# Graph attention layer on one core: ScalarE's queue asks for the right halves of x after GpSimd's first constant, and the first weight slab is asked for after the second left half

## The chip, the cores and the metric

The program runs on one core of a Trainium2 chip. Its engines are TensorE (PE), VectorE (DVE), ScalarE (ACT), GpSimd (POOL) and SyncE (SP); transfers are asked for on the queues of SP, ACT and POOL and are all carried by the core's 16 DMA engines. The metric is device time in microseconds of one execution, as the median of several runs.

## What is computed

x has 384 rows (nodes) of 1024 features. The kernel normalises each row, applies relu, runs a graph attention layer with 16 heads on it and adds the result to x:

```
h = relu(layernorm(x))                                 # 384 x 1024
q, k, v = h @ wq.T + bq, h @ wk.T + bk, h @ wv.T + bv
q2, k2, v2 = q @ wiq.T + biq, k @ wik.T + bik, v @ wiv.T + biv     # split into 16 heads of 64
mask[src, dst] = softplus(edge_type_weights)[type - 1]  # -inf elsewhere, 6528 edges
attn = softmax(q2 @ k2.T / 8 + mask)
out = x + (attn @ v2) @ wo.T + bo
```

## The kernel before

The seven weight matrices come as 56 slabs of 128 x 1024 float32 (512 KB each), in the order in which TensorE uses them. Every slab and every activation is split into a high and a low part (w_hi, w_lo; a_hi, a_lo), and each product is three matmuls: high by high, low by high, high by low. ScalarE makes the high parts, VectorE or GpSimd the low ones. Each engine has its own program, written out by hand in order; semaphores tie them together, and nothing is scheduled by a planner.

The change touches the start alone, which runs so:

- SyncE (L286 on) asks for the left halves of x's three tiles, `x_sb[:, t, 0:512]`, 256 KB each (L289). Then follow the slabs (L305): slab 0 once the first left half has landed (L304); slab 1; then the weights of the edge types, the biases, the rows and columns of the edges (L307 to L312); slab 2; two fills of the table in memory that the mask is scattered into (`cells<-prob`, L316); slab 3 once slab 0 has been split; and so on, three raw slabs at a time.
- ScalarE (L450 on) asks for the three right halves of x (L470) as its first work. Then it loads a table, turns tiles 0 and 1 of x into h (relu with scale and bias, L476), makes the high part of the left half of slab 0 (L467), scales tile 2 in two quarter pieces (L482), and takes the eight turned blocks of h from PSUM as a_hi (L486), with slab 1's high part between (L456).
- GpSimd (L342 on) writes its constants: `iota` first (L345), which raises the semaphore iota_ok, then `above`, `ident` and others, and fills two blocks (L363). Then it raises each tile's variance to the power -1/2 (rstd, L367), and makes the low parts of slab 0 (L384) and slab 1 (L374).
- VectorE (L598 on) makes the statistics of each half of each tile as it lands (L679), left half first; the aggregate (L683) and the variance plus epsilon (L685) after both; and the shift of the tile before (L626) after the left half of the next. Of tile 2 it does the subtraction itself (L689, L693), converts the right half of slab 0 (L695), and makes a_lo (L725).
- TensorE (L845 on) waits for iota and above and runs 18 warming matmuls (L890), turns seven of the eight blocks of tile 0 (L894), runs 4 warming ones, turns tile 1, runs 3, turns tile 2, and starts the first tile of v (L922, L923, L929). After it come all other tiles and slabs (L849 to L851) and the heads.

Of the kernel before, what the change touches and what calls it, by code (L numbers as in the profile page):

```python
# [66 lines left out]
def tiles_of(group):  # L67
    return range(group * EG, min((group + 1) * EG, ET))


def gat_kernel(nc, slabs, x, edge_cols, edge_rows, edge_weights, biases, bo, out):
    with ExitStack() as ctx:
# [3 lines left out]
        def sem(name):  # L76
            return ctx.enter_context(nc.semaphore(name))
# [71 lines left out]
        def key_copy(pos):  # L149

            first, n = [(work2, 0), (work2, 4), (work2, 8), (work, 0), (work, 4), (work, 8), (prob, 19), (prob, 23),
                        (prob, 3), (prob, 7), (prob, 11), (prob, 15), (prob, 0)][pos], len(tiles_of(UNIT_ORDER[pos])) * P
            flat = prob[:, :, :, :].rearrange("p a t n -> p (a t n)") if first[0] is prob else first[0]
            return flat[:, first[1] * P:first[1] * P + n]

        def cell_rows(c):

            return cells[c][0:N * N, :].rearrange("(t p n) a -> p t (n a)", p=P, n=N)
# [18 lines left out]
        x_in = [[sem(f"x_in{t}_{b}") for b in range(2)] for t in range(NT)]  # L177
        slab_in = [sem(f"slab_in{r}") for r in range(RAW)]
        const_step, iota_ok, above_ok = sem("const_step"), sem("iota_ok"), sem("above_ok")
# [81 lines left out]
        def wait_lo(eng, s):  # L261

            eng.wait_ge(slab_lo_dve if lo_by_vector(s) else slab_lo, lo_count(s))
# [22 lines left out]
        @block.sync  # L286
        def _(sp_eng):
            for t in range(NT):
                sp_eng.dma_start(x_sb[:, t, 0:HALF], x[t * P:(t + 1) * P, 0:HALF]).then_inc(x_in[t][0], 16)  # L289
            def load_keys(pos):  # L290

                unit = UNIT_ORDER[pos]
                part = key_rows[0:1, unit * EG * P:(unit * EG + len(tiles_of(unit))) * P]
                sp_eng.dma_start(key_copy(pos), part.to_broadcast([P, len(tiles_of(unit)) * P])).then_inc(
                    keys_in[pos], 16)

            for s in range(SLABS):
                if s >= RAW:

                    wait_lo(sp_eng, s - RAW)  # L300
                    if s == RAW:
                        sp_eng.wait_ge(half_lo, 1)
                if s == 0:
                    sp_eng.wait_ge(x_in[0][0], 16)  # L304
                sp_eng.dma_start(raw[:, s % RAW, :], slabs[s]).then_inc(slab_in[s % RAW], 16)  # L305
                if s == 1:
                    sp_eng.dma_start(ew[:], edge_weights.rearrange("(a n) -> a n", a=1).to_broadcast([P, 4])).then_inc(  # L307
                        ew_in, 16)
                    sp_eng.dma_start(bias[:], biases).then_inc(small_in, 16)
                    for i in range(2):  # L310
                        sp_eng.dma_start(rows_i[:, i, :], edge_rows[i * DST_ROW:i * DST_ROW + ET, :]).then_inc(rows_in, 16)
                    sp_eng.dma_start(cols_i[:], edge_cols).then_inc(edges_in, 16)  # L312
                if s == 2:
                    for c in range(2):
                        sp_eng.wait_ge(fill_ok, c + 1)
                        sp_eng.dma_start(cell_rows(c), prob[:, c]).then_inc(filled, 16)  # L316
                if s == 4:
                    sp_eng.wait_ge(key_row_ok, 1)
                    sp_eng.dma_start(key_rows[0, :].rearrange("(t e) -> t e", e=P), key_row[:]).then_inc(keys_out, 16)
                if 6 <= s < 4 + GROUPS:  # L320
                    if s == 6:
                        sp_eng.wait_ge(keys_out, 16)
                    elif s == 10:
                        sp_eng.wait_ge(filled, 32)
                    if s < 8:
                        load_keys(2 * (s - 6))
                        load_keys(2 * (s - 6) + 1)
                    else:
                        load_keys(s - 4)
                if s == Q0 + 2:  # L330

                    sp_eng.wait_ge(h_turned, KT)
                    sp_eng.wait_ge(later_ok, 3 * EG)
                    for t in range(NT):
                        sp_eng.dma_start(y[:, t, :], x[t * P:(t + 1) * P, :]).then_inc(y_in, 16)
                    sp_eng.dma_start(bo_sb, bo.rearrange("(a n) -> a n", a=1).to_broadcast([P, F])).then_inc(y_in, 16)
            for i, (_, n, cols_out, _) in enumerate(out_pieces):
                sp_eng.wait_ge(out_ok, i + 1)
                sp_eng.dma_start(out[n * P:(n + 1) * P, cols_out], y[:, n, cols_out]).then_inc(stored, 16)
            sp_eng.wait_ge(stored, 16 * len(out_pieces))  # L340
# [110 lines left out]
        def _(act):  # L451
# [6 lines left out]
            def tile_hi_part(t):  # L458
                hi, _, b, psum = tile_place(t)
                act.wait_ge(slab_used, slab_of(t) + 1)  # L460
                nc.scalar.activation(hi, psum[:, 0:N], ACT.Identity, bias=bias[:, b:b + 1]).then_inc(tile_hi, 1)  # L461

            def first_slab_hi():
# [2 lines left out]
                act.wait_ge(slab_in[0], 16)  # L466
                nc.scalar.activation(w_hi[:, 0, half], raw[:, 0, half], ACT.Copy).then_inc(half_hi, 1)  # L467

            for t in range(NT):
                act.dma_start(x_sb[:, t, HALF:F], x[t * P:(t + 1) * P, HALF:F]).then_inc(x_in[t][1], 16)  # L470
            for t in range(NT):
# [127 lines left out]
        def _(dve):  # L599
# [241 lines left out]
            for i, (_, n, cols_out, psum) in enumerate(out_pieces):  # L841
                dve.wait_ge(out_done, i + 1)
                nc.vector.tensor_tensor(y[:, n, cols_out], psum, y[:, n, cols_out], ALU.add).then_inc(out_ok, 1)
# [283 lines left out]
```

## Time and profile before

| | us |
|---|---|
| median of three runs (295.4 to 295.67) | 295.45 |
| the profiled execution | 295.47 |
| its span, from the first to the last instruction | 293.7 |
| TensorE busy | 287.4 |
| VectorE, ScalarE, GpSimd busy | 176.7, 153.5, 150.7 |

The span is what the trace covers; the profiled execution's own time is 1.77 us longer. A row of the time line gives an instruction's or a run of instructions' start and length in us from the start of the span, the engine (PEld is TensorE's weight load, SPq and ACTq are the instructions with which SyncE and ScalarE ask for a transfer), the line, the output and the input, how many were merged, and in brackets the idle time ahead of it and what ended it. For a transfer, the trace also has the time from the instruction that asks for it to its landing, the moment at which its semaphore is raised.

### The profile page before, as it was taken

To read this page: it belongs to the slowest core of one execution; us is meant where nothing else is said; L and a number is where in the kernel's file an instruction comes from. 1 tells how busy PE (TensorE), PEld (TensorE's weight loads), DVE (VectorE), ACT (ScalarE), POOL (GpSimd) and SP (SyncE) were. 2 spreads that over 40 slices of the span, in tenths; PEclk is the share of its full clock that TensorE was granted. 3 is DMA by queue.
4 is the path that set the end of the run, shared out by engine and by line. 5 is a ranking of instruction groups with operands and counts; after the bars stand their busy time and mean duration, and the time that the engine had idled before them with its cause. 6 is when DMAs were issued, how large, how long until landed. Compare 5 with 4: busy or idle time off the path is not lost.

```text
span 293.7 us, 4994 instructions
## 1 busy us (share of the span) xinstructions
PE 287.4 (98%) x1813; PEld 266.4 (91%) x1813; DVE 176.7 (60%) x475; ACT 153.5 (52%) x288; POOL 150.7 (51%) x153
## 2 busy tenths in 40 slices
PE   6899999999999999999999999999999999999996
PEld 3699998888899999999999999999999997888885
DVE  4999778786544534454467766665747475835241
ACT  2876443152523443244324685969687879874100
POOL 6552455543464455545300797758393939874000
PEclk9999999999999999999999999999999999999999
DMA  7978955749733443334654043140403132400032
GB/s 257 332 230 264 315 191 180 232 153 301 270 105 117 139 143 136 91 134 145 182 193 145 0 141 106 46 144 0 145 10 136 41 106 71 144 1 2 0 143 71
DMA packets 15818, 40.84 MB, mean 139 GB/s; under 512 B 3481, under 2 KB 4914, under 8 KB 15794
## 3 DMA queue, kind: packets, MB, share of 16 engines
q1 hardware_dynamic: 13346, 38.53, 39.2%
q0 software_dynamic: 2016, 1.21, 1.8%
q10 hardware_dynamic: 432, 0.79, 0.7%
q8 instruction: 14, 0.23, 0.3%
q14 instruction: 10, 0.08, 0.1%
HBM read 37.71 MB, written 2.81 MB: 138 GB/s over the span
## 4 chain that ended last, share of the span: by engine, by line
PE 95%; DMA 2%; ACT 1%; DVE 0%; SPq 0%; issue 0%
PE banks L849 27%; PE banks L850 26%; PE banks L851 26%; PE banks L966 5%; PE banks L1009 3%; PE banks L1010 3%; PE banks L981 3%; DMA x_sb<-in_x 2%; PE banks L994 1%; PE banks L894 1%; PE banks L922 1%; PE banks L929 0%; PE banks L923 0%; ACT x_sb L476 0%; SPq L289 0%; DVE stats L679 0%
## 5 line engine op out<-in xcount | busy, mean ns | idle before, releaser
L403 POOL DMA_INDIRECT cells<-value,cell x51 | 54.8, 1074 | 59.2 <-DMA cells<-value,cell 45.9
L456 ACT ACTIVATE w_hi<-raw 128x1024 fp32r<-128x1024 f32 x51 | 53.8, 1055 | 17.5 <-PE banks L851 17.3
L849 PE MATMUL banks<-a_hi,w_hi 128*128 128x384 f32 x184 | 61.5, 334 | 0.0
L850 PE MATMUL banks<-a_hi,w_lo 128*128 128x384 f32 x184 | 61.5, 334 | 0.0
L851 PE MATMUL banks<-a_lo,w_hi 128*128 128x384 f32 x184 | 61.5, 334 | 0.0
L712 DVE TENSOR_TENSOR w_lo<-raw,w_hi 128x1024 fp32r<-128x1024 f32 x36 | 44.0, 1223 | 12.6 <-ACT w_hi L456 12.5
L429 POOL TENSOR_SCALAR prob<-prob,row_inv 128x384 f32<-128x384 f32 x36 | 22.5, 640 | 43.6 <-DVE row_inv L779 43.6
L374 POOL TENSOR_TENSOR w_lo<-raw,w_hi 128x1024 fp32r<-128x1024 f32 x15 | 36.0, 2404 | 0.9 <-ACT w_hi L456 0.9
L849 PEld LDWEIGHTS banks<-a_hi,w_hi 128*128 128x128 f32 x184 | 34.5, 188 | 0.1
L850 PEld LDWEIGHTS banks<-a_hi,w_lo 128*128 128x128 f32 x184 | 34.5, 188 | 0.0
L851 PEld LDWEIGHTS banks<-a_lo,w_hi 128*128 128x128 f32 x184 | 34.5, 188 | 0.0
L783 DVE TENSOR_TENSOR pt_lo<-banks,pt_hi 128x384 fp32r<-128x384 f32 x48 | 23.8, 551 | 13.3 <-ACT pt_hi L548 13.1
L461 ACT ACTIVATE b_hi<-banks,bias 128x384 fp32r<-128x384 f32 x16 | 9.3, 581 | 35.0 <-PE banks L851 35.0
L534 ACT ACTIVATE prob<-prob,neg_max 128x384 f32<-128x384 f32 x36 | 21.8, 606 | 9.2 <-DVE neg_max L769 9.2
L548 ACT ACTIVATE pt_hi<-banks 128x384 fp32r<-128x384 f32 x48 | 20.1, 491 | 5.6 <-PE banks L1010 4.5
L849 PE MATMUL banks<-c_hi,w_hi 128*128 128x384 f32 x64 | 22.2, 346 | 0.0
L700 DVE SCALAR_TENSOR_TENSOR b_lo<-banks,bias,b_hi 128x384 fp32r<-128x384 f32 x16 | 9.9, 617 | 20.1 <-ACT b_hi L461 20.1
L849 PE MATMUL banks<-b_hi,w_hi 128*128 128x384 f32 x64 | 21.9, 343 | 0.0
L851 PE MATMUL banks<-b_lo,w_hi 128*128 128x384 f32 x64 | 21.4, 335 | 0.0
L851 PE MATMUL banks<-c_lo,w_hi 128*128 128x384 f32 x64 | 21.4, 334 | 0.0
L850 PE MATMUL banks<-c_hi,w_lo 128*128 128x384 f32 x64 | 21.4, 334 | 0.0
L850 PE MATMUL banks<-b_hi,w_lo 128*128 128x384 f32 x64 | 21.4, 334 | 0.0
(146 smaller groups left out, 610.1 us busy)
## 6 DMA issues: line engine op xcount, KB each, us to landing
raw<-in_slabs SPq DMA_DIRECT2D x56, 512.0 KB, 3.4
work<-key_rows SPq DMA_DIRECT2D x6, 256.0 KB, 5.3
prob<-key_rows SPq DMA_DIRECT2D x6, 256.0 KB, 3.8
x_sb<-in_x SPq DMA_DIRECT2D x3, 512.0 KB, 6.0
out_y<-x_sb SPq DMA_DIRECT2D x5, 256.0 KB, 2.1
cells<-prob SPq DMA_DIRECT2D x2, 576.0 KB, 7.9
cells<-value,cell POOLq DMA_INDIRECT x51, 2.6
x_sb<-in_x ACTq DMA_DIRECT2D x3, 256.0 KB, 4.3
```

The source lines that it names most:

```text
L374: nc.gpsimd.tensor_tensor(lo, raw[:, s % RAW, :], hi.bitcast(F32), ALU.subtract).then_inc(slab_lo, 1)
L403: nc.gpsimd.indirect_dma_start(out=cells[c][:, :], out_offset=bass.IndirectOffsetOnAxis(ap=cell[:, t:t + 1], axis=0), in_=value[:, t:t + 1 ...
L429: nc.gpsimd.tensor_scalar(probs[j % 2][x][:, n, :], probs[j % 2][x][:, n, :], row_inv[:, j % 2, c:c + 1], 1.0, ALU.mult, ALU.mult).then_in ...
L456: nc.scalar.activation(split_place(s)[0], raw[:, s % RAW, :], ACT.Copy).then_inc(slab_hi, 1)
L534: nc.scalar.activation(probs[j % 2][x][:, n, :], probs[j % 2][x][:, n, :], ACT.Exp, scale=-1.0, bias=neg_max[:, j % 2, c:c + 1], accum_out ...
L548: nc.scalar.activation(pt_as_placed(pt_hi, h, m), pt_place(h, m), ACT.Copy).then_inc(pt_hi_ok, 1)
L712: nc.vector.tensor_tensor(lo, raw[:, s % RAW, :], hi.bitcast(F32), ALU.subtract).then_inc(slab_lo_dve, 1)
L783: nc.vector.tensor_tensor(pt_as_placed(pt_lo, h, m), pt_place(h, m), pt_as_placed(pt_hi, h, m).bitcast(F32), ALU.subtract).then_inc(pt_lo_ ...
L849: nc.tensor.matmul(psum, w[0], a[0], start=first, stop=False)
L850: nc.tensor.matmul(psum, w[1], a[0], start=False, stop=False)
L851: return nc.tensor.matmul(psum, w[0], a[1], start=False, stop=last)
L966: mm = nc.tensor.matmul(score_bank(2 * n + x)[:, 0:N], q[own, turn, m], k[own, turn, :], start=(p == 0), stop=(p == 2))
```

## The change

ScalarE waits for iota_ok, GpSimd's first constant, before it asks for the right halves of x. SyncE waits for the second left half of x instead of the first before it asks for slab 0. The line numbers from there on are two higher in the changed kernel for ScalarE's part below the wait and everything after it.

```
@@ -301,7 +301,7 @@
                     if s == RAW:
                         sp_eng.wait_ge(half_lo, 1)
                 if s == 0:
-                    sp_eng.wait_ge(x_in[0][0], 16)
+                    sp_eng.wait_ge(x_in[1][0], 16)
                 sp_eng.dma_start(raw[:, s % RAW, :], slabs[s]).then_inc(slab_in[s % RAW], 16)
@@ -466,6 +466,8 @@
                 act.wait_ge(slab_in[0], 16)
                 nc.scalar.activation(w_hi[:, 0, half], raw[:, 0, half], ACT.Copy).then_inc(half_hi, 1)
 
+
+            act.wait_ge(iota_ok, 1)
             for t in range(NT):
                 act.dma_start(x_sb[:, t, HALF:F], x[t * P:(t + 1) * P, HALF:F]).then_inc(x_in[t][1], 16)
```

ScalarE at the start of the program, before (x_sb<-in_x is a right half of x, w_hi<-raw the high part of slab 0's left half):

```order
L470 DMA x_sb<-in_x 128x512 x3
L476 ACT_TABLE_LOAD
L476 ACTIVATE x_sb<-x_sb,shift,rstd 128x1024 [waits shift_ok] x2
L467 ACTIVATE w_hi<-raw 128x512 [waits slab_in0]
L482 ACTIVATE x_sb<-x_sb,rstd 128x256 [waits rstd_ok,h_step]
```

And in the changed kernel:

```order
L472 DMA x_sb<-in_x 128x512 [waits iota_ok]
L472 DMA x_sb<-in_x 128x512 x2
L478 ACT_TABLE_LOAD
L478 ACTIVATE x_sb<-x_sb,shift,rstd 128x1024 [waits shift_ok] x2
L467 ACTIVATE w_hi<-raw 128x512 [waits slab_in0]
L484 ACTIVATE x_sb<-x_sb,rstd 128x256 [waits rstd_ok,h_step]
```

The order of the instructions is the same; the first request now carries a wait, and the two others and all else on ScalarE stand behind it.

SyncE at the start of the program, before (x_in0_0 is raised when the left half of tile 0 has landed, x_in1_0 that of tile 1; raw<-in_slabs is a weight slab):

```order
L289 DMA x_sb<-in_x 128x512 x3
L305 DMA raw<-in_slabs 128x1024 [waits x_in0_0]
L305 DMA raw<-in_slabs 128x1024
L307 DMA ew<-in_edge_weights 128x4
L309 DMA bias<-in_biases 128x48
```

And in the changed kernel:

```order
L289 DMA x_sb<-in_x 128x512 x3
L305 DMA raw<-in_slabs 128x1024 [waits x_in1_0]
L305 DMA raw<-in_slabs 128x1024
L307 DMA ew<-in_edge_weights 128x4
L309 DMA bias<-in_biases 128x48
```

The order is the same here too; slab 0 waits for another landing, and everything that SyncE asks for afterwards stands behind that wait.

## Rows read from the trace of the kernel before

**Rows 1.** Busy time in stretches: length, PE, PEld, DVE, ACT, POOL, granted clock, DMA share, GB/s.

```profile
0.00:12.00 12.00, 8.51 (x43) 4.82 (x43) 7.43 (x18) 5.73 (x8) 6.99 (x20) 1.00 0.79 271
12.00:290.00 278.00, 277.90 (x1764) 260.79 (x1765) 168.80 (x457) 147.75 (x281) 143.68 (x133) 1.00 0.41 135
```

**Rows 2.** The chain of waits: start, us, what.

```profile
1.70 6.04 DMA x_sb<-in_x
...
8.55 1.25 ACT x_sb L476
...
12.10 0.41 PE banks L922
```

**Rows 3.** Time line of VectorE, its first instructions.

```profile
3.98 1.29 DVE L679 BATCH_NORM_STATS2 stats<-x_sb 128x6 f32<-128x512 f32 x2 [3.98 <-DMA x_sb<-in_x]
...
6.39 0.16 DVE L626 SCALAR_TENSOR_TENSOR shift<-mean_var,rstd 128x1 f32<-128x1 f32 x1
6.47 0.69 DVE L679 BATCH_NORM_STATS2 stats<-x_sb 128x6 f32<-128x512 f32 x1
...
7.76 0.69 DVE L679 BATCH_NORM_STATS2 stats<-x_sb 128x6 f32<-128x512 f32 x1 [0.18 <-DMA x_sb<-in_x]
8.37 0.14 DVE L626 SCALAR_TENSOR_TENSOR shift<-mean_var,rstd 128x1 f32<-128x1 f32 x1
8.43 0.69 DVE L679 BATCH_NORM_STATS2 stats<-x_sb 128x6 f32<-128x512 f32 x1
```

**Rows 4.** Requests for x, left (L289), right (L470): ns, first and last start; landing.

```profile
L289 SPq DMA_DIRECT2D x_sb<-in_x x3: 382/417/424, 0.8 to 1.7; - x3
...
DMA to landing us min/median/max: 3.2/4.2/6.0
...
L470 ACTq DMA_DIRECT2D x_sb<-in_x x3: 404/455/455, 0.8 to 1.7; - x3
...
DMA to landing us min/median/max: 3.3/4.3/6.2
```

**Rows 5.** The table by stretches again, its weakest microsecond under x.

```profile
5.00:6.00 1.00, 1.00 (x5) 0.48 (x4) 0.93 (x4) 0.00 (x0) 0.22 (x1) 1.00 0.86 266
```

**Rows 6.** Time line of GpSimd: iota, three rstd, slab 0's low half, first scatter.

```profile
0.90 0.45 POOL L345 IOTA iota<- 128x384 f16 x1 [0.40 <-POOLq L1121]
...
5.78 0.57 POOL L367 TENSOR_TENSOR rstd<-var_eps,minus_half 128x1 f32<-128x1 f32 x1 [1.22 <-DVE var_eps L685]
7.67 0.55 POOL L367 TENSOR_TENSOR rstd<-var_eps,minus_half 128x1 f32<-128x1 f32 x1 [1.31 <-DVE var_eps L685]
9.63 0.75 POOL L367 TENSOR_TENSOR rstd<-var_eps,minus_half 128x1 f32<-128x1 f32 x1 [1.41 <-DVE var_eps L685]
10.39 1.28 POOL L384 TENSOR_TENSOR w_lo<-raw,w_hi 128x512 fp32r<-128x512 f32 x1
...
22.30 1.26 POOL L396 DMA_INDIRECT cells<-sp,self_cell  x1 [3.20 <-issue]
```

**Rows 7.** Time line of ScalarE and TensorE up to the first tile.

```profile
6.59 1.24 ACT L476 ACTIVATE x_sb<-x_sb,shift,rstd 128x1024 f32<-128x1024 f32 x1 [3.11 <-DVE shift L626]
...
9.70 0.62 ACT L467 ACTIVATE w_hi<-raw 128x512 fp32r<-128x512 f32 x1
...
10.48 0.91 ACT L482 ACTIVATE x_sb<-x_sb,rstd 128x256 f32<-128x256 f32 x2 [0.16 <-POOL rstd L367]
...
11.15 0.73 PE L894 MATMUL banks<-ident,x_sb 128*128 128x128 f32 x4
...
15.39 1.13 ACT L456 ACTIVATE w_hi<-raw 128x1024 fp32r<-128x1024 f32 x1
```

**Rows 8.** Requests for slab 0 and slab 2 (L305): us from each to its landing.

```profile
DMA to landing us min/median/max: 5.1/5.1/5.1
...
DMA to landing us min/median/max: 6.6/6.6/6.6
```

**Rows 9.** Requests for the two fills (L316): us to landing.

```profile
DMA to landing us min/median/max: 7.4/7.9/8.5
```

More of the change, by code:

```diff
@@ L303, in _ @@
                 if s == 0:
-                    sp_eng.wait_ge(x_in[0][0], 16)
+                    sp_eng.wait_ge(x_in[1][0], 16)
                 sp_eng.dma_start(raw[:, s % RAW, :], slabs[s]).then_inc(slab_in[s % RAW], 16)
@@ L467, in first_slab_hi @@
                 nc.scalar.activation(w_hi[:, 0, half], raw[:, 0, half], ACT.Copy).then_inc(half_hi, 1)
+            act.wait_ge(iota_ok, 1)
             for t in range(NT):
```

## The prediction

> **What bounds the kernel now.** I read the busy time in stretches of the span first. TensorE is busy for 8.51 of the first 12 us and for all but a tenth of a microsecond of the 278 us that follow [rows 1]: past 12 us nothing but the stream of matmuls counts. A change of the start moves the end by as much as it moves the first matmul of the first tile (L922, at 12.10 us), and by nothing else, unless a later consumer runs dry. The granted clock is 1.00 in both stretches.
>
> The chain of waits then tells what sets those 12.10 us [rows 2]: SyncE asks for the third left half of x at 1.70, which lands 6.04 us later at 7.74; VectorE makes its statistics and the shift of the second tile; ScalarE's relu of that tile starts at 8.55; seven transposes, three warming matmuls and a_hi lead to L922. VectorE's time line shows how narrowly the landing leads [rows 3]: VectorE works without a break from 3.98 us on and stands idle for only 0.18 us ahead of the third left half. So two things bind nearly equally: the first two landings, which start VectorE's chain, and the third left half.
>
> I write L0, L1, L2 for the left halves (SyncE's queue) and R0, R1, R2 for the right ones (ScalarE's). The left ones land 3.2, 4.2 and 6.0 us after they are asked, the right ones 3.3, 4.3 and 6.2, each queue asking at 0.8 to 1.7 us [rows 4]. That is L0 at 3.97, R0 at 4.09, L1 at 5.43, R1 at about 5.5, L2 at 7.74, R2 at about 7.9. Two halves are down by 4.1 and four by 5.5, so one half (256 KB) costs 0.7 us of the shared DMA engines. The last pair takes 2.3 us instead of 1.4 because slab 0, asked at 3.97, is served beside it: 0.9 us lost.
>
> **The change, part by part.** The sum is made against the profiled execution: span 293.7, time 295.47, so 1.77 us outside the span; the median of the runs shown is 295.45, 0.02 below.
>
> *R0 is asked later.* GpSimd's first constant, the iota, runs from 0.90 for 0.45 us [rows 6], so ScalarE is released at 1.35 and asks at about 1.40 instead of 0.79: 0.61 later, and all three right halves with it. What the landing does isn't in the trace. Upper end: L0 and L1 are both asked before, R0 is the third half, and the line through two halves (4.05) and four (5.47) gives 4.76. Lower end: a half next to another takes 3.3 us; without its 0.7 us of company 2.6, so 4.0. Plain shift: 4.09 + 0.61 = 4.70. I take 4.70, as L1 (asked at 1.23) is certain to be in the engines together with R0, which is the case that the row of 3.3 us measured. L0 now lands alone and some 0.7 us earlier, at about 3.3, which gives nothing: VectorE's mean needs R0. The statistics of R0 start now at 5.27 less 0.69, thus 4.58 [rows 3]; with R0 at 4.70 they start at 4.72. That moves VectorE's, GpSimd's and ScalarE's chain of the first tile by **+0.14 us** (ends: -0.6 and +0.2).
>
> *L2 is no longer late.* With slab 0 asked later and the right halves behind, L2 is the fourth or fifth half: 5.5 to 6.2, and 6.5 if it fares like the weak stretch of 5 to 6 us, 266 GB/s [rows 5], which makes one half cost 1.0 us. VectorE wants it at 7.58 + 0.14. So the 0.18 us of idle time is gone in every case. What is late next is rstd of the second tile: GpSimd ends it at 7.67 + 0.55 = 8.22 [rows 6], and the first shift followed its rstd by 0.04 (5.78 + 0.57 = 6.35, then 6.39). So the shift can stand at 8.26 instead of 8.37: **-0.11 us**, no more.
>
> *R1.* VectorE wants it at 6.47 + 0.14 = 6.61. It is the fifth half at the latest: 5.5 + 0.7 = 6.2, or 6.5 in the weak stretch. Cost nothing, with 0.1 to 0.4 us of cover.
>
> *R2.* Wanted at 8.43, and 8.46 by the two terms above. It is last: 5.5 + 1.4 = 6.9 if slab 0 stayed away, and 8.3 with all of slab 0 (two halves' worth, 1.4 us) in front. Behind R2 hang rstd of the last tile, then ScalarE's quarter pieces (L482, from 10.48, the first done at about 10.98), while TensorE comes to their transposes only at 11.15 [rows 7]: another 0.17 us of cover. I take nothing.
>
> *The first slab.* It is asked when L1 has landed, which is 4.6 to 4.8 (4.76 as the third half), not 3.97; 0.7 to 0.8 later. Now it takes 5.1 us and lands at 9.07 [rows 8]; but its packets stood behind L2 anyway, so it needn't lose all of that. If it does, it lands at 9.87. ScalarE's first half of the split (L467) starts now at 9.70 and takes 0.62; it would then end at 10.51, against 10.48 where the quarter pieces start, for which GpSimd's rstd is waited until 9.63 + 0.75 = 10.38 anyway [rows 6, 7]. So 0.03 us of the 0.17 us of cover. GpSimd's low half would start at 10.55 instead of 10.39 and end at 11.83 [rows 6], and TensorE wants it behind L922 at 12.10. Cost nothing; without that cover it would be up to 0.2.
>
> *What is queued behind the new waits.* On SyncE all later requests go up to 0.8 us later. The tightest is slab 2: asked after 7.3, 6.6 us to its landing at 13.9, used by ScalarE at 15.39, a slack of 1.5 [rows 7, 8]. The fills take 7.4 and 8.5 us from 7.75 and some 8.2, so 16.7 at the latest; GpSimd's first scatter, which wants them, starts at 22.30 [rows 6, 9]. On ScalarE the other two right halves and a table load stand behind its wait; ScalarE is idle for 3.11 us ahead of the first relu [rows 7], so 0.61 us of it is there to lose. Nothing.
>
> Sum: +0.14 - 0.11 = +0.03 us on 295.47: 295.50, and by the median 295.48. I give **295.5 us**.
>
> A rule of the skill bears on the first term. The halves land in pairs 0.1 to 0.2 us apart [rows 4], as if the queues took turns. The Trainium skill, "DMA: Bandwidth & Descriptors", section "Queues, rings and completion order", says that each DMA engine goes round the queues by whole packets of some 9 to 17 descriptors; a half has 128 rows over 16 engines, 8 each, so by that rule one half would be one turn. L1 would then go wholly before R0. It would be the second half (4.05) and R0 the third (4.76), the first term +0.20 and the sum +0.09; slab 0 would be asked at 4.07, nearly as now. The pairs agree with the rule and with a finer sharing alike.
>
> **The rivals.**
> (a) *A small gain.* R0 comes at 4.4 or earlier because L0 is out of the engines when R0's rows enter. Then the first term is 0.0 or negative down to -0.3 and the second stays: -0.1 to -0.4, 295.05 to 295.35. For it: L0 is alone on the engines for its first 0.6 us, most of one half's 0.7. Against it: L1, asked 0.17 us before R0. Chance 0.25.
> (b) *The right halves starve; the other side.* R0 to R2 are 0.61 us later while SyncE's queue runs ahead with L2 and then 512 KB slabs, whose rows are twice as long; if the queues take turns row by row, R2 gets a third of the engines and needs 2.1 us instead of 0.7. It decides from the moment that R2 lands after 8.46 + 0.17 = 8.63, or R1 after 6.61. From R2's 6th place without a slab (6.9) and 1.4 us of slab 0 that makes 8.3; with slab 1 mixed in (another 1.4 us at most) 9.7, and then 9.7 - 8.63 = 1.07 us: 296.0 at half of it, 296.6 at the end. For it: slab 0 took 0.9 us from the last pair already. Against it: both waits hold slab 0 back by as much as the right halves. Chance 0.15, of which the part over 0.59 us is 0.05.
> (c) *The change does nothing that can be seen*, since R0 at 4.6 and a gain of 0.1 meet: that is the forecast's own neighbourhood, +-0.15 us. Chance of the forecast 0.58.
> (d) Anything that I don't see, such as TensorE's pause ahead of the first transposes growing by 0.14 and costing clock. Its granted clock is 1.00 over the first 12 us, that pause among them [rows 1]. Chance 0.02.
>
> **How the numbers follow.** Forecast 295.35 to 295.65, likeliest 295.5. Leaving out the lowest tenth (half of (a)'s reach) and the highest (the worse two thirds of (b)) gives 295.15 to 295.85. A measurement of this kernel tells about 0.2%, 0.59 us, from no change. Below 294.86 only a first term near its lower end would lead: 0.03. Above 296.04 the last part of (b) and (d): 0.06. Within: 0.91.
>
> **What would show it.** R0's statistics (second of L679) at 4.7; no idle time ahead of L2's; the shift of the second tile within 0.1 of 8.4; ScalarE's relus at 6.73 and 8.58; L922 at 12.05 to 12.2; slab 0 asked at 4.7 and landed before 9.9, with no idle time on ScalarE ahead of L467; TensorE's busy time from 12 to 290 us unchanged. Wrong would be: R0 landed below 4.4 or above 4.9, VectorE idle ahead of R1 or R2, or TensorE idle anywhere past 12.5 us.

## The result and the profile after

| | before | changed |
|---|---|---|
| median, us | 295.46 (six runs, 295.4 to 295.67) | 297.54 (six runs, 296.85 to 299.7) |
| profiled execution | 295.47 | 299.16 |
| its span | 293.7 | 297.4 |
| first matmul of the first tile | 12.10 | 15.74 |

The ratio is 1.0083, with a 95% interval of 1.0061 to 1.0105. The change makes the kernel 0.8% slower, which lies outside the range of the prediction, and it spreads its six runs over 3 us where the six of before lie within 0.3. The spread is not the changed kernel's alone: of 87 more runs of the kernel before, taken beside the experiments, 79 lie from 295.27 to 295.99 us and eight from 296.52 to 299.94.

In the profiled execution the span grows by 3.7 us and the first matmul comes 3.64 us later, so all of its loss is made before it. Once it has started, TensorE waits nowhere else up to 290 us. This execution is one of the three longer ones (298.03, 299.16 and 299.7 us, mean granted clock 0.993 to 0.994); the other three took 296.85 to 297.06 us at a clock of 0.999 or 1.000, and no trace shows how late R0 was in them. So the two parts of the loss read below are those of the longer runs, and the medians differ by only 2.1 us.

The chain of waits of the changed kernel, from its first request for a right half on (start, us, what), answers to [rows 2]. The names L0, L1, L2 and R0, R1, R2 are those of the prediction, for the left and right halves of the three tiles:

```profile
1.38 5.96 DMA x_sb<-in_x
7.34 0.03 issue
7.37 0.70 DVE stats L681
...
8.57 0.58 POOL rstd L367
9.16 0.02 issue
9.18 0.17 DVE shift L628
9.35 0.03 issue
9.38 1.25 ACT x_sb L478
10.63 0.14 issue
10.76 1.73 PE banks L896 x7
12.49 1.22 PE banks L892 x4
13.71 0.76 PE banks L896 x7
14.47 0.49 PE banks L892 x3
```

R0, not L2, now leads the chain. It is asked at 1.38 as foreseen, and takes 5.96 us to its landing at 7.34 instead of 3.3. Everything behind it in the first tile's normalisation moves with it: R0's statistics from 4.58 to 7.37 and the first relu from 6.59 to 9.38, both 2.79 later. The other 0.85 of the 3.64 us is in TensorE's rows: seven transposes take 1.73 us, and the four warming matmuls 1.22.

VectorE's time line shows the same wait (against [rows 3]), and how early L0 now is:

```profile
3.43 0.69 DVE L681 BATCH_NORM_STATS2 stats<-x_sb 128x6 f32<-128x512 f32 x1 [3.43 <-DMA x_sb<-in_x]
7.37 0.69 DVE L681 BATCH_NORM_STATS2 stats<-x_sb 128x6 f32<-128x512 f32 x1 [3.24 <-DMA x_sb<-in_x]
```

The requests for the halves (us to landing: smallest, median, largest), against [rows 4]:

```profile
L289 SPq DMA_DIRECT2D x_sb<-in_x x3: 382/421/424, 0.8 to 1.7; - x3
...
DMA to landing us min/median/max: 2.6/3.5/5.8
...
L472 ACTq DMA_DIRECT2D x_sb<-in_x x3: 381/450/453, 1.4 to 2.3; - x3
...
DMA to landing us min/median/max: 6.0/6.3/6.5
```

Before, the two queues landed their halves in step. Now all three right halves need 6.0 us or more, the left ones 2.6, 3.5 and 5.8.

The table by stretches (length, PE, PEld, DVE, ACT, POOL, granted clock, DMA share, GB/s), first before, then changed:

```profile
3.00:4.00 1.00, 1.00 (x4) 0.44 (x3) 0.02 (x1) 0.47 (x1) 1.00 (x2) 1.00 1.06 377
...
10.00:13.00 3.00, 2.78 (x20) 2.18 (x20) 2.89 (x5) 2.76 (x8) 2.29 (x3) 1.00 0.93 331
```

```profile
3.00:4.00 1.00, 1.00 (x4) 0.44 (x3) 0.57 (x1) 1.00 (x1) 1.00 (x2) 1.00 0.80 219
...
10.00:13.00 3.00, 2.24 (x10) 1.87 (x11) 2.83 (x9) 2.38 (x3) 1.24 (x2) 0.52 0.94 309
```

From 3 to 4 us the DMA engines move 219 GB/s instead of 377, although L1 and L2 and all right halves have been asked for. From 10 to 13 us TensorE's granted clock is 0.52 in the mean, nearly all of it at the lower of its two levels (1.2 GHz instead of 2.4), where TensorE had stood still for 3.16 us, up to 10.76. So the loss has two parts: a late R0, 2.8 us, and the clock, some 0.85 us, both of which the forecast had put aside.

The packets by queue tell whose requests the engines serve (packets, MB, share of 16 engines). q10 is ScalarE's queue: it carries 0.79 MB in the whole span, the three right halves, and q1 is SyncE's. From 2 to 3 us, before:

```profile
q1 hardware_dynamic: 78, 0.16, 44.5%
q10 hardware_dynamic: 72, 0.15, 40.3%
```

In the changed kernel q10 has no packet at all in that microsecond, though R0 is asked at 1.38:

```profile
q1 hardware_dynamic: 156, 0.29, 82.2%
```

From 4 to 7 us it is the other way round: ScalarE's queue moves more than two halves and SyncE's less, and still R0 isn't whole:

```profile
q10 hardware_dynamic: 315, 0.58, 57.5%
q1 hardware_dynamic: 174, 0.34, 41.1%
```

So R0 is not waiting all that time for SyncE's queue to finish. What it waits for is taken up below, under "Which part of R0 is late".

### The profile page after: what moved, and what is told of

Its sections match the earlier page's. It is cut to its first block, busy times and chain, and to the rows that moved or that the text cites. A ratio compares the mean times of both kernels' runs of the same rounds, so it can differ in the third digit from the quotient of the medians.

```text
span 297.4 us, 4994 instructions
## 1 busy us (share of the span) xinstructions
PE 288.6 (97%) x1813; PEld 267.5 (90%) x1813; DVE 176.8 (59%) x475; ACT 153.6 (52%) x288; POOL 149.8 (50%) x153
## 4 chain that ended last, share of the span: by engine, by line
PE 95%; DMA 2%; ACT 1%; DVE 1%; POOL 0%; issue 0%; POOLq 0%
PE banks L851 27%; PE banks L853 26%; PE banks L852 26%; PE banks L968 5%; PE banks L1011 3%; PE banks L1012 3%; PE banks L983 3%; DMA x_sb<-in_x 2%; PE banks L996 1%; PE banks L896 1%; PE banks L892 1%; PE banks L924 1%; PE banks L931 0%; PE banks L925 0%; ACT x_sb L478 0%
```

## The experiments

I name a request's delay behind L0's request its gap. The kernel before has a gap of 0.0 us (R0 at 0.79, L0 at 0.79), the changed one 0.58. "First matmul" is always that of the first tile, in the profiled execution.

**The two halves of the change.** Slab 0 alone:

```
-                    sp_eng.wait_ge(x_in[0][0], 16)
+                    sp_eng.wait_ge(x_in[1][0], 16)
```

> The change's second half alone: SyncE asks for slab 0 after L1, ScalarE does not wait. In the changed kernel R0 is asked at 1.38 us and lands at 7.34 instead of 4.09, and the first matmul of the first tile starts at 15.74 instead of 12.10. Theory Q (queue order: R0 to R2 fall behind SyncE's L1 and L2, because they are asked after them): R0 lands at 4.1 as before, slab 0 is asked at about 5.4, L2 lands a bit earlier than 7.74, time 295.3 to 295.5, the same as before. Theory S (the postponed slab is to blame, what it now meets delays the last halves and the first split): R0 at 4.1 too, but slab 0 lands after 9.7 and the time is 296 or more.

Measured: 295.88 us median of ten runs, ratio 1.0026 (1.0010 to 1.0043); ratios are always to the kernel before, with the 95% interval in brackets. Six runs are at 295.40 to 295.97, four at 296.85 to 297.44. The profiled one is of the first kind: R0 takes 3.5 us, and by the table of stretches the halves now fill the engines from 5 to 6 us, where [rows 5] had the weak stretch:

```profile
5.00:6.00 1.00, 1.00 (x5) 0.49 (x4) 0.93 (x4) 0.00 (x0) 0.03 (x1) 1.00 1.06 401
```

L2 takes 5.4 us instead of 6.0 and VectorE is no longer idle ahead of it; but L0 landed 0.2 later in this profile, and the first matmul stands at 12.19. It gains nothing, and something costs 1.4 us in four runs of ten, which is taken up below.

The wait alone:

```
+            act.wait_ge(iota_ok, 1)
             for t in range(NT):
                 act.dma_start(x_sb[:, t, HALF:F], ...)
```

> The change's first half alone: ScalarE waits for iota before its three requests, SyncE asks for slab 0 after L0 as before. Theory Q: R0 lands at 7 to 8 us, as in the changed kernel (7.34), and the time is that of the changed kernel or more, 297 to 300, because slab 0 is now asked at about 3.4 and stands in SyncE's queue beside the right halves. Theory S: R0 lands by 5 us and the time is within 0.3 us of 295.5.

Measured: 299.65 us (297.35 to 300.56, four runs), ratio 1.013 (1.0076 to 1.0183). R0 takes 5.6 us and lands at 7.0, and the first matmul is at 15.69. So the wait alone makes the whole loss, and slab 0 has no part in R0's lateness. Theory S fell. That the median is 2 us above that of the full change stays open; it has only four runs, and the intervals overlap.

**The clock by itself.** The changed kernel with more warming matmuls:

```
-WARM = [18, 4, 3]
+WARM = [29, 4, 3]
```

> The changed kernel with 29 warming matmuls instead of 18 ahead of the first transposes, so that TensorE is not idle from 7.6 to 10.8 us. In the changed kernel the granted clock was 0.92 in the first 12 us and 0.91 in the next 8, after a pause of 3.16 us, and seven transposes took 1.73 us instead of 0.98. If the time lost is 2.8 us of late R0 (first relu at 9.38 instead of 6.59) and about 0.85 us of clock, this kernel has a clock of 1.00 throughout, R0 still at about 7.3, L922's successor at about 14.9 and a time of about 298.3 where the changed one has 299.1. If the clock is not a cause of its own, the time is that of the changed kernel.

Measured: 297.32 us median of five runs (296.7, 296.76, 297.32, 301.85 and 302.81), ratio 1.0051 (1.0031 to 1.0071). In the profiled run R0 landed at 7.3 as in the changed kernel, and TensorE's time line shows a pause of 1.15 us ahead of the transposes:

```profile
10.72 0.96 PE L896 MATMUL banks<-ident,x_sb 128*128 128x128 f32 x7 [1.15 <-ACT x_sb L478]
11.52 0.81 PE L892 MATMUL banks<-iota,above 128*128 128x384 f16 x4
```

The clock is 1.00 up to 20 us, the seven transposes take 0.96 us again, and the first matmul comes at 14.75 instead of 15.74: between these two profiles 1.0 us was the clock's, and 2.65 us are R0's. The run times don't confirm that price: the medians are 0.2 us apart and the runs of the two kernels overlap. This profile is of the run of 301.85 us, in which TensorE also waited 2.1 us at its first scores because VectorE waited for the mask; the clock fell once more there (0.96 in the mean from 140 to 180 us). In the view of waits (us, times, longest):

```profile
DVE prob L719 <- DMA prob<-cells: 4.7, 1, 4.7
```

**Is it the scatters too?** In the kernel before, VectorE waits 0.3 us at that place, so I asked whether the scatters that build the mask are nearly critical. Twelve memsets were put ahead of the first one in the kernel before:

```
+                    for r in range(12 * (1 - c)):
+                        if r:
+                            pool.wait_ge(idle_ok, r)
+                        nc.gpsimd.memset(idle[:], float(r)).then_inc(idle_ok, 1)
```

> The kernel before, with twelve small memsets (about 3 us in all) on GpSimd ahead of the first scatter, on a tile that nobody reads; nothing at the start of the program changes. In the first experiments a run in which the scatters took longer had TensorE idle for 2.1 us at the first scores, VectorE waiting 4.7 us for the mask, where it waits 0.3 us in the kernel before. Theory M (TensorE's cover at that place is 4.4 - 2.1 = 2.3 us, and the scatters' pace varies from run to run): VectorE waits about 3.3 us, TensorE is idle for about 0.7 us at its first scores and the median is 296.0 to 296.5, with a wider spread than before. If the scatters are not near the critical path, the time stays at 295.5 and TensorE idles nowhere after 12.5 us.

Measured: 295.37 us (295.26 to 295.8, ten runs), ratio 0.9992 (0.9976 to 1.0008): nothing. The first scatter moved from 22.30 to 24.86, but the first one that carries an edge waits for VectorE's cells and moved from 29.16 to 29.57 only, as GpSimd's time line has it:

```profile
24.86 1.46 POOL L402 DMA_INDIRECT cells<-sp,self_cell  x1 [0.20 <-issue]
29.57 1.31 POOL L409 DMA_INDIRECT cells<-value,cell  x1 [3.25 <-DVE cell L656]
```

So a later start of the scatters costs nothing. But the test made the mask no later: the last scatter starts at 139.91 us as against 139.88 before, and VectorE waits 0.4 us for it. Whether slower scatters, theory M, are behind some of the long runs was therefore not tested. In the one profile with the wait of 4.7 us they were slower (49.6 us of waiting for them against 45.9).

**Why is R0 late? The order of the requests.** First R0 no later than L1: SyncE too waits for iota before L1 and L2.

```
             for t in range(NT):
+                if t == 1:
+                    sp_eng.wait_ge(iota_ok, 1)
                 sp_eng.dma_start(x_sb[:, t, 0:HALF], ...)
```

> The changed kernel, and SyncE too waits for iota before L1 and L2, so that R0 is asked no later than L1. Theory Q: R0 lands at 4 to 5 us, since it stands beside L1 again and not behind L1 and L2; the time is 295.5 to 296. The rival, theory D (a request made at 1.4 us meets something that one made at 0.8 does not, whatever the order: GpSimd's fill from 2.5 to 4.6 us, the table load): R0 still lands after 6.5 us and the time is 297 or more.

Measured: 297.02 us (296.61 to 297.45), ratio 1.0048 (1.0031 to 1.0065). R0 takes 5.0 us and lands at 6.44, between the two expectations. (TensorE's pause was 2.92 us here, and its clock stayed at 1.00.) Then L1 behind R0: the same wait on `const_step`, GpSimd's second constant, with a third request order L0, R0, L1.

> The changed kernel, and SyncE asks for L1 and L2 only after GpSimd's second constant (1.51 us), so the order of the requests is L0 0.8, R0 1.38, L1 about 1.56. In the run with L1 asked at 1.4 beside R0, R0 took 5.0 us; in the changed kernel, with L1 asked 0.15 us ahead of R0, it took 5.96; with all halves 0.6 us later it took 3.4. Theory Q2 (R0 is late because L1's request was taken first): R0 takes 3.2 to 3.6 us and lands by 5.0; first matmul at about 12.6, time 295.9 to 296.2 in undisturbed runs. Rival A (what counts is that R0 comes 0.6 us behind its partner L0, whatever L1 does): R0 again takes 5 us or more, time 297.

Measured: 297.68 us (296.34 to 304.47, eight runs), ratio 1.0066 (1.0030 to 1.0103). R0 takes 5.5 us though L1 is asked behind it, at 1.53; VectorE's time line:

```profile
6.93 0.69 DVE L683 BATCH_NORM_STATS2 stats<-x_sb 128x6 f32<-128x512 f32 x1 [2.81 <-DMA x_sb<-in_x]
```

Theory Q2, the order of R0 and L1, fell here. What if R0 keeps its time and only R1 and R2 wait, and what if all six move together? First, ScalarE waits only ahead of R1 and R2:

```
             for t in range(NT):
+                if t == 1:
+                    act.wait_ge(iota_ok, 1)
                 act.dma_start(x_sb[:, t, HALF:F], ...)
```

> The changed kernel, but ScalarE waits for iota only after it has asked for R0: R0 goes out at 0.8 us, R1 at about 1.38 instead of 1.25, R2 at 1.8. Theory Q2 (what hurts is that R0's request comes after SyncE's L1 and shares a serial stage with it, so R0's rows reach the engines more than 2 us after the request): R0 lands at 4.0 to 4.3, the first relu starts at 6.6 to 6.9, the time is 295.4 to 296. Theory D (requests in flight at 1.4 us and later are slow for all): R1 lands after 7 us and the time is 296.5 or more.

Measured: R0 takes 3.5 us and the first matmul is at 12.16. R1, now asked at 1.38, takes 4.5 us and lands at 5.9: a request at 1.38 is not late by itself. The median of ten is 296.21 us with a ratio of 1.0022 (1.0001 to 1.0044): five runs at 295.55 to 295.88, four at 296.54 to 297.1 and one at 300.51, much as with slab 0 alone, which is asked after L1 here too. In the second, SyncE waits for iota ahead of L0, so that all six move by 0.6 us:

```
+            sp_eng.wait_ge(iota_ok, 1)
             for t in range(NT):
                 sp_eng.dma_start(x_sb[:, t, 0:HALF], ...)
```

> The changed kernel, with SyncE waiting for iota too before L0: all six halves are asked for 0.6 us later than in the kernel before, in the same order among each other. Theory Q2: the picture of before returns, shifted: L0 and R0 land at 4.6 to 4.8 us, the first matmul starts at about 12.7 and the time is 296.0 to 296.2. Theory D: R0 lands after 6 us, time 297 or more.

Measured: 296.94 us (296.03 to 298.1, ten runs), ratio 1.0042 (1.0019 to 1.0065). L0 takes 3.2 us and R0 3.4, asked at the very time at which R0 is slow in the changed kernel. So theory D fell too: nothing that happens at 1.4 us is to blame. What is left is the gap between L0's and R0's requests.

**The size of the gap.** A short wait, for GpSimd's smallest constant made first (with slab 0 after L1 here):

```
+            nc.gpsimd.memset(minus_half[:], -0.5).then_inc(const_step, 1)
             nc.gpsimd.iota(iota[:], ...)
...
+            act.wait_ge(const_step, 1)
             for t in range(NT):
                 act.dma_start(x_sb[:, t, HALF:F], ...)
```

> The changed kernel with a shorter wait: GpSimd's smallest constant (minus_half, 0.09 us long) is made ahead of iota and releases ScalarE at about 1.0 us, so R0 is asked at about 1.05, behind L0 (0.8) but before L1 (1.23). Theory Q2: R0 keeps its place before L1 and lands at 4.2 to 4.5; time 295.4 to 296. Rival P (the loss grows in proportion to the delay, 3.2 us for 0.6 us): R0 lands at about 5.4 and the time is 296.3 to 297.

Measured: asked at 0.92, R0 takes 3.3 us, lands at 4.2, and the profiled run is at 295.08. The median of ten is 296.47 (295.08 to 300.93), ratio 1.0022 (0.9976 to 1.0067): unclear. Five of the ten are at 297.11 or more, and the two longest, 299.34 and 300.93, have no profile and no explanation. The same with slab 0 after L0 again, as in the kernel before:

> The kernel before with the short wait alone: ScalarE asks for R0 at 0.92 us instead of 0.79 (behind GpSimd's smallest constant), slab 0 after L0 as before. With both waits this landed R0 at 4.2 and L0 at 3.6, and the fastest runs were 295.08, 0.4 below the kernel before, with others at 297 to 301. Theory Q2 + W (the gain comes from L0 having the engines first, the runs of 297.1 to 297.5 from slab 0's late request, those of 299 and more from R0 falling behind L1 in some executions): runs at 295.0 to 295.2 and some at 299 or more, none near 297.3; median 295.1. If the 0.12 us changes nothing, all runs are at 295.3 to 295.8.

Measured: **295.07 us** median of eleven (294.94 to 295.32), ratio 0.9986 (0.9977 to 0.9995), with none of the late runs that were half expected. R0, asked at 0.92, takes 3.6 us, and the first matmul is at 11.93. With the constant `above` made first instead, asked at 1.02, gap 0.22:

> ScalarE released by the constant above, made first on GpSimd: R0 asked at about 1.1 us, 0.3 behind L0 and 0.1 ahead of L1; slab 0 after L0 as before. Gaps so far: 0.0 us, R0 takes 3.3 to 3.4; 0.12 us, 3.6; 0.58 us, 5.0 to 6.0. Theory A (the gap between L0's and R0's requests decides, and grows into the late landing step by step): R0 takes 4.2 to 4.8, lands at 5.3 to 5.9, time 296 to 297. Rival T (there is a threshold, the first 0.3 us are free): R0 takes 3.6 or less and the time is 294.9 to 295.3.

Measured: 295.2 us (295.06 to 295.85), ratio 0.9987 (0.9974 to 1.0). R0 takes 3.3 us; there is no growth up to here, so theory A's step by step is wrong. Between 0.22 and 0.58 us nothing was measured. And the other side, a gap of 1.5 us, with ScalarE waiting for above_ok:

> ScalarE waits for above (2.3 us) instead of iota, so R0 is asked at 2.3, after L0, L1 and L2; slab 0 after L0. If the right halves just come behind all left ones, whenever they are asked (theory C), R0 still lands near 7 to 7.5 us, a time of 5 us, and the kernel is at 297 to 300 as with the 0.6 us gap. If the loss grows with the gap, R0 lands after 8.5 and the time is 299 to 302.

Measured: 299.29 us (298.65 to 300.16), ratio 1.0136 (1.0117 to 1.0155). R0 is asked at 2.34 and takes 4.2 us, less than with the gap of 0.6, and lands at 6.6; the other two take 6.5 and 7.0 (ScalarE's requests, then their landings):

```profile
L472 ACTq DMA_DIRECT2D x_sb<-in_x x3: 378/450/457, 2.3 to 3.2; - x3
...
DMA to landing us min/median/max: 4.2/6.5/7.0
```

**Whose queue, and whose company.** The queues exchanged: SyncE waits for iota ahead of L0, ScalarE doesn't wait.

> The two queues change places: SyncE waits for iota before L0, L1, L2 (asked from 1.38), ScalarE asks at 0.8 as in the kernel before, slab 0 after L0. Theory A with equal queues: the later queue is served late whichever it is, L0 takes 5 to 6 us and lands after 6.4, R0 lands at 3.4; time 297 or more. Rival Z (it is ScalarE's queue that suffers): L0 takes 3.4 us and lands at 4.8, time 295.7 to 296.2.

Measured: 298.96 us (297.46 to 299.45), ratio 1.0106 (1.0071 to 1.014). Now L0 is slow, 4.7 us, and R0 fast, by the requests of both queues:

```profile
L290 SPq DMA_DIRECT2D x_sb<-in_x x3: 382/417/424, 1.4 to 2.3; - x3
...
DMA to landing us min/median/max: 4.7/5.3/5.3
...
L471 ACTq DMA_DIRECT2D x_sb<-in_x x3: 379/450/455, 0.8 to 1.7; - x3
...
DMA to landing us min/median/max: 2.6/3.7/5.3
```

So the delay falls on the later queue, whichever it is. Last, ScalarE's wait as in the change, but L1, L2, R1 and R2 are asked for only after R0 has landed:

```
+                if t == 1:
+                    sp_eng.wait_ge(x_in[0][1], 16)      # the same on ScalarE
```

> ScalarE waits for iota as in the changed kernel, but nothing else is in flight: L1, L2 and R1, R2 are asked for only after R0 has landed; slab 0 after L0. If R0's 5 to 6 us come from the company of the other halves (theory C, L1 and L2 are served ahead of it on some engines), R0 takes 2.6 to 3.0 us here and lands at 4.0 to 4.4, though slab 0 is asked at 3.4. If the gap to L0 itself is what costs (a stage that is slow to take up the second queue), R0 takes 5 us here too. The time says nothing, as L1 to R2 are asked 3 us later than before: 297 to 299.

Measured: R0, asked at 1.38, has landed at 4.1, and VectorE's time line shows it going from L0 to R0 without a break (x2 is both halves):

```profile
3.51 1.29 DVE L685 BATCH_NORM_STATS2 stats<-x_sb 128x6 f32<-128x512 f32 x2 [3.51 <-DMA x_sb<-in_x]
```

ScalarE's three requests in that kernel, R0 the smallest:

```profile
L476 ACTq DMA_DIRECT2D x_sb<-in_x x3: 366/378/456, 1.4 to 4.5; - x3
...
DMA to landing us min/median/max: 2.7/3.5/4.9
```

The gap to L0 alone does no harm; R0 is slow only in the company of the other halves. Which of the four it is, L1 and L2 or R1 and R2, was not separated. (The time, 298.32, says nothing here.)

**Which part of R0 is late.** The landing of a half is the last of 16 raises of its semaphore; the kernel waits for 16, as in `wait_ge(x_in[0][0], 16)`. The traces hold the time of each raise, so they tell whether R0 comes late as a whole or in single parts. All in us from the start of the span:

| kernel | R0 asked | first part | 14th | 16th |
|---|---|---|---|---|
| before | 0.79 | 3.79 | 4.06 | 4.13 |
| gap 0.12, slab 0 after L0 | 0.92 | 4.04 | 4.30 | 4.48 |
| changed | 1.38 | 4.73 | 5.38 | 7.34 |
| L1 asked behind R0 | 1.38 | 3.90 | 5.14 | 6.91 |
| L0 and R0 alone | 1.38 | 3.73 | 3.93 | 4.09 |

In the changed kernel R0 is asked 0.59 us later than before. Its first part is down at 4.73, which is 0.35 us more than that shift, and the 14th at 5.38, 0.73 us more. The last two come at 6.80 and 7.34, and everything that needs R0 waits for them: of the 2.6 us that R0 lands after a plain shift, some 1.9 us are theirs. By then ten parts of R1 and six of R2, asked later on the same queue, are down. First and last part of R0 lie 1.8 to 3.0 us apart in the five kernels with a gap of 0.58 in company, 1.3 to 1.4 for the late half at a gap of 1.5 us and with the queues exchanged, and 0.3 to 0.5 in all eleven others. A late start alone doesn't make it: the first packet of ScalarE's queue comes 2.4 us after R0's request in the changed kernel and 1.3 before, but at a gap of 0.12 it comes 2.1 after, and R0 is in time.

**What slab 0 costs.** With slab 0 after L1, four of ten runs took 1.4 us more. The one profile in which a late slab 0 shows is that of the kernel with all halves 0.6 us later (298.1 us, first matmul at 14.74). There slab 0, asked at 5.94, let ScalarE wait, by its time line:

```profile
12.66 0.63 ACT L468 ACTIVATE w_hi<-raw 128x512 fp32r<-128x512 f32 x1 [2.30 <-DMA raw<-in_slabs]
```

Two runs test it. Slab 0 later still, after L2 (`x_in[2][0]`):

> The kernel before, with slab 0 asked for after L2 has landed (about 7.1 to 7.7 us) instead of after L0 (3.97). Six of twenty runs with slab 0 asked at about 5.5 were 1.0 to 1.9 us slower than the rest, and in the one profile that shows such a loss (all halves 0.6 us later, slab 0 asked at 5.94) ScalarE waited 2.3 us for slab 0. Theory W (slab 0's landing becomes the bound when it is asked late, and sometimes does already at 5.5): slab 0 lands at 11.5 to 13 here, ScalarE is idle ahead of L467 by 2 to 3 us, the time is 297.5 to 298.5 in every run. If slab 0 still had cover, the time stays at 295.5 to 296.

Measured: 296.68 us median, ratio 1.0055 (1.0031 to 1.0078); five of seven runs at 296.28 to 296.72, the others at 298.05 and 298.94. Asked at 7.12, slab 0 made ScalarE wait 0.54 us, for it took 3.3 us now that L2 was out of the way, and the first matmul is at 12.53. The direction is that of theory W; the wait is a quarter of what I expected, and the loss of 1.2 us about half. And slab 0 after L0 as before, with slab 1 and all behind it after L1:

```
+                if s == 1:
+                    sp_eng.wait_ge(x_in[1][0], 16)
```

> The kernel before, with slab 0 asked after L0 as before and only slab 1 (and with it everything behind it on SyncE) held until L1 has landed. Theory W says that the slow runs of the version with slab 0 after L1 come from slab 0 itself: here they are gone and the spread is that of the kernel before, median 295.4 to 295.6. If the requests behind it (slabs 1 and 2, fills) are what costs, the slow runs of 296.8 to 297.4 remain.

Measured: 295.47 us, ten runs of 295.27 to 295.75, ratio 0.9993 (0.9980 to 1.0006). The times of 296.85 and above are gone. Taken together, the three kernels with R0 in time and slab 0 after L1 (slab 0 alone, only R1 and R2 waiting, the short wait) have 14 of 30 runs above 296.5 us, and the four with slab 0 after L0 and R0 in time (this one, the scatters, gaps 0.12 and 0.22) none of 41. So it is slab 0's own late request that goes with the long runs, not those behind it. That they come from ScalarE's wait for it is argued from the one profile above; the kernel before has such runs too, eight of 87.

## Why the prediction was wrong, point by point

- *What bounds the kernel*: right. All that the change did in the profiled run was done before the first matmul, and the loss there (3.64 us) is that of the span (3.7).
- *R0 is asked later, +0.14 us, ends -0.6 and +0.2*: this is the step that failed. The request came at 1.38 as worked out; the landing was 7.34 and not 4.70, and the term +2.79. The upper end of 4.76 was a bound by bandwidth: the third half can't come later than three halves' worth of transfer. That supposed engines which are always busy and serve in the order asked, and a half that moves as one piece. Measured against the plain shift of 4.70, fourteen of R0's sixteen parts came up to 0.7 us late, down by 5.38, and the last two at 6.80 and 7.34; a landing is that of the last part. The row of 3.3 us had been measured with both queues asking at the same moment, and the statement that L1 beside R0 "is the case that the row of 3.3 us measured" was wrong in just that point. At gaps of 0.12 and 0.22 us it still held (3.3 to 3.6 us); at 0.58 it took 5.0 to 6.0 in five kernels.
- *The rule of the skill* that each DMA engine goes round the queues by whole packets (the Trainium skill, "DMA: Bandwidth & Descriptors", section "Queues, rings and completion order") gave, by the prediction's estimate, 4.76 for R0. The trace does not bear that number out: R0 landed at 7.34 with two halves asked before it.
- *L2 no longer late, -0.11 us*: not to be seen in the changed kernel, where VectorE wants L2 at 10.29, long after its landing. In the kernel with slab 0 alone L2's idle time went as worked out, and the second relu, at 8.64, is where 8.55 less 0.11 and the 0.19 us by which L0 landed later put it; the first matmul (12.19) came no earlier for that later L0. But L2 landed at 7.1 there and not at 5.5 to 6.5, although slab 0 stayed away until 5.6, so of the 0.9 us put down to slab 0 at most 0.7 were its own.
- *R1, R2, the first slab, what is queued behind*: no wait for any of them shows in the changed kernel, but in part only since all else was 2.8 us later: slab 0 landed at 10.0, where ScalarE had begun on it at 9.70 before. That slab 0 was asked at 4.74 (forecast 4.76) is luck: L1 was the second half down and not the third. With R0 on time its late request went with a loss of 1.0 us or more in four runs of ten, which I had put at "cost nothing" from one profile of the kernel before.
- *Rival (a), a small gain*, had L0 out of the engines when R0's rows enter. L0 did come early, at 3.4 (forecast 3.3), and the late parts of R0 undid it. The gain of its size came at a gap of 0.12 us.
- *Rival (b), the right halves starve*, named the side that loses but set it at R2 and slab 0, with 8.63 us as the point from which it decides. It was R0 that came late, with slab 0 at either place, and not for want of its queue's share: ScalarE's queue moved 0.58 MB from 4 to 7 us and SyncE's 0.34.
- *Rival (d), TensorE's pause and its clock*, was given 0.02 and a growth of 0.14 us. The pause grew to 3.16 us and the clock fell to 0.52 from 10 to 13 us; the profile with 29 warming matmuls puts a price of 1.0 us on it.

## What to carry to other kernels

A transfer's time to landing holds for the pattern of requests in which it was measured: where two queues asked within 0.22 us of each other, both halves landed 2.8 to 3.6 us after their requests; where they were split by 0.6 us with more requests behind, the later one took 5.0 to 6.0 us, at a price of 2 to 3 us for 256 KB. What came more than 1 us behind the first part was one to three of the sixteen parts of that half, so a landing is a matter of its slowest part and not of the mean rate. A bound by bandwidth is a lower bound for the landing and not an upper one, so where a change moves requests against each other, the upper end of its range has to come from a run. If the first work of a program waits for both halves of a tile, let both queues ask within 0.2 us of each other. A delay of 0.12 us gave 295.07 us here, 0.14% below the kernel before, and one of 0.22 us 295.2 us, an interval that reaches up to no change. That the gain comes from the delay is argued: L0 landed at 3.6 to 3.9 us in these profiles and at 4.0 to 4.2 in those without a delay, but GpSimd's constants were also written in another order.

## What the runs showed of the hardware

- Time from request to landing of the first half of the later queue: 3.3 to 3.6 us at gaps of 0 to 0.22 us (all kernels with such a gap, before among them), 5.0 to 6.0 at 0.58 us (the changed kernel and four others), 4.2 at 1.5 us, 4.7 when SyncE's queue is the later one, and 2.7 at 0.58 us where of the other halves only its partner was asked for.
- The lateness is that of single parts of the transfer: in the changed kernel 14 of the 16 raises of R0's semaphore lie from 4.73 to 5.38 us, the last two at 6.80 and 7.34. Before, all 16 lie from 3.79 to 4.13.
- Until the late queue's packets come the engines are not full: 219 GB/s and a share of 0.80 from 3 to 4 us in the changed kernel, 377 and 1.06 before. While its last parts are awaited they are: 307 GB/s and 0.99 from 4 to 7 us, against 335 and 0.95 before.
- Why single parts stay behind in company stays open. The order of R0 and L1, GpSimd's or ScalarE's work at 1.4 us, the place of slab 0 and the identity of the queue are excluded as causes. The traces don't say which DMA engine carried a part, so whether the late ones belong to the same engine each time, and what it did meanwhile, can't be read from them.
- Where TensorE stood still for 3.16 us its granted clock was 0.52 in the mean from 10 to 13 us, the lower level for nearly all of it. So it was with pauses of 2.69 us (the wait alone, 0.56) and 2.77 us (L1 behind R0, 0.50), but not with one of 2.92 us (L1 and L2 waiting for iota too) nor with one of 1.15 us, where it stayed at 1.00. The length of the pause alone did not decide it.
